# ViT block with experts on one core: second statistics on ScalarE, a new hand-written order of units, products on a constant at two waits

## What is computed

```python
h = tokens(x)                              # 16x16 patches @ W + b, a class token, position codes
h = h + attn(layernorm(h))                 # linear attention with running sums (cumsum) over the tokens
u = layernorm(h)
gates = softmax(u @ w_router + b_router); topv, topi = top_k(gates, 2)
pos = cumsum(one_hot(topi)) - 1; keep = pos < cap          # cap = 185 tokens per expert
buf[e, pos] += u[token]                    # gather the tokens of each expert
out = gelu(buf @ w1[e] + b1[e]) @ w2[e] + b2[e]
h = h + sum(w * out[e, pos]) / sum(w)      # w = the gates of the choices that are kept
```

## Time and profile before

| | us |
|---|---|
| three runs, median (lowest, highest) | 168.11 (167.69, 168.73) |
| profiled execution, its own time | 169.34 |
| profiled execution, span from the first to the last instruction | 167.5 |
| busy: TensorE, VectorE, ScalarE, GpSimd | 157.5, 111.4, 77.4, 51.7 |

### The profile page before, as it was taken

The page is one execution under the profiler, slowest core; times in us unless marked ns, Lnnn a source line. Parts: engine busy times, 40 slices in busy tenths (PEclk is TensorE's granted clock), DMA queues, the critical chain, the costliest instruction groups (busy, mean ns, idle before and its releaser), DMA issues.

```text
span 167.5 us, 3069 instructions
## 1 busy us (share of the span) xinstructions
PE 157.5 (94%) x1041; PEld 148.2 (88%) x1041; DVE 111.4 (67%) x361; ACT 77.4 (46%) x186; POOL 51.7 (31%) x51
## 2 busy tenths in 40 slices
PE   7999999999999789989989999999999999999960
PEld 7679999986886689979989999999999999999950
DVE  0077673688588998396948876948669486694620
ACT  4306543526452309343705737657365583655300
POOL 2006213043021000000721735627266272703351
PEclk9999999999999955899999999999999999999995
DMA  5999930096014410620158789887888868820422
GB/s 164 429 411 420 386 125 0 9 337 206 0 29 134 122 45 4 195 59 4 45 175 308 144 287 268 248 266 137 287 253 255 263 145 276 245 22 6 46 25 22
DMA packets 17264, 28.48 MB, mean 170 GB/s; under 512 B 1289, under 2 KB 13875, under 8 KB 17125
## 3 DMA queue, kind: packets, MB, share of 16 engines
q1 hardware_dynamic: 14789, 25.48, 45.2%
q0 software_dynamic: 2464, 2.86, 10.0%
HBM read 24.20 MB, written 4.14 MB: 169 GB/s over the span
## 4 chain that ended last, share of the span: by engine, by line
PE 77%; DVE 14%; issue 2%; POOL 2%; DMA 1%; POOLq 1%; DVEq 0%
PE ps L1170 21%; PE ps L1193 11%; PE ps L1091 7%; PE ps L1076 6%; PE ps L1030 6%; PE ps L1195 5%; PE ps L1011 4%; DVE prod L777 2%; DVE z_s L775 2%; PE ps L1203 2%; PE ps L1042 2%; DVE onehot L752 2%; PE ps L1180 2%; PE ps L1158 2%; DMA rows_in<-xrows,src_row 1%
## 5 line engine op out<-in xcount | busy, mean ns | idle before, releaser
L475 POOL DMA_INDIRECT out_rows<-out_s,dst_row x16 | 23.7, 1483 | 40.4 <-ACT out_s L620 34.1
L596 ACT ACTIVATE first_t<-ps,b_cur 128x186 f32<-128x186 f32 x64 | 23.1, 412 | 25.5 <-PE ps L1170 25.5
L1193 PE MATMUL ps<-hid_hl,split 128*128 128x372 f32 x96 | 29.0, 369 | 0.0
L460 POOL DMA_INDIRECT rows_in<-xrows,src_row x14 | 15.7, 1124 | 33.2 <-DVE src_row L868 29.2
L1195 PE MATMUL ps<-hid_hl,split 128*128 128x186 f32 x96 | 23.9, 249 | 0.0
L1170 PE MATMUL ps<-first_t,w_even 128*128 128x186 f32 x128 | 21.8, 322 | 0.7 <-DVE first_t L890 0.7
L1170 PE MATMUL ps<-first_t,patch_t 128*128 128x186 f32 x128 | 21.6, 321 | 0.0
L899 DVE CAST hid_hl<-first_t 128x372 fp32r<-128x372 f32 x28 | 10.7, 383 | 16.1 <-ACT first_t L596 16.1
L1170 PEld LDWEIGHTS ps<-first_t,w_even 128*128 128x128 f32 x128 | 20.1, 190 | 1.0 <-issue 1.0
L1170 PEld LDWEIGHTS ps<-first_t,patch_t 128*128 128x128 f32 x128 | 20.1, 190 | 0.0
L1195 PEld LDWEIGHTS ps<-hid_hl,split 128*128 128x128 f32 x96 | 18.3, 191 | 0.0
(11 more groups left out here) (165 smaller groups left out, 272.9 us busy)
## 6 DMA issues: line engine op xcount, KB each, us to landing
w_even<-w SPq DMA_DIRECT2D x8, 1024.0 KB, 5.3
patch_t<-w SPq DMA_DIRECT2D x8, 1024.0 KB, 5.3
patch_t<-patches SPq DMA_DIRECT2D x2, 972.0 KB, 11.2
att<-attn SPq DMA_DIRECT2D x1, 1280.0 KB, 8.4
first_t<-first SPq DMA_DIRECT2D x1, 870.0 KB, 6.0
xrows<-xn SPq DMA_DIRECT2D x3, 288.0 KB, 2.4
out_rows<-h SPq DMA_DIRECT2D x3, 288.0 KB
first_t<-first SPq DMA_DIRECT2D x1, 580.0 KB, 4.2
```

Of the source, the lines that this page charges most:

```text
L460: pool.indirect_dma_start(out=rows_in[q][0:SIZES[s], s, :], out_offset=None, in_=xrows[:, :], in_offset=bass.IndirectOffsetOnAxis(ap=src_r ...
L475: pool.indirect_dma_start(out=out[:, :], out_offset=bass.IndirectOffsetOnAxis(ap=dst_row[0:SIZES[s], c:c + 1], axis=0), in_=out_s[q][0:SIZ ...
L596: ins = act.activation(hid[:, f, :], bank(pair)[:, (f % 2) * SL:(f % 2 + 1) * SL], ACT.Gelu, bias=b1_cur[q][:, f:f + 1])
L1193: pe.matmul(dst[:, 0:2 * SL], w2_h[q][:, f, cols], hid_hl[:, f].rearrange("p a s -> p (a s)"), start=f == 0, stop=False)
```

## The change

- The mean of the second normalisation comes from the router product: `wr_c` has a ninth column of 1/256, set by GpSimd, and `means2` on VectorE copies nine columns per tile to `read_s`. The sum of squares about that mean comes from ScalarE: one ACTIVATE Square per tile with `accum_out` (`squares2`), whose elements go to `xn` and are overwritten by `rows2`. `root2` takes it with a scale of 1/256. `bn_stats` and `bn_aggr` of norm2 are gone.
- `UNITS`, the PSUM slots, `DVE_ORDER`, `ACT_ORDER` and GpSimd's order are new. norm2 E comes before norm2 C, both before slots 0. pick 0 and pick 1 are units in slot 0.
- `rows2` and `keep2` count as two steps; SyncE stores `xn` and `h2` each after its own, in ScalarE's order.
- Four products on the constant stand before slots 0, three before pick 0 (`bridge`).
- pick 1 runs over its five tiles for the first half of the features, then for the second; each half is signalled.
- In expert 0 the look-up of ids comes after pair 2; down half 1 is cut after six of its eight blocks, and the look-up of weights and `turn_in` stand in the cut. The biases of expert 0 are copied at the start.

The diff, cut to its core:

```diff
+BRIDGES = {('slots', 0): 4, ('pick', 0): 3}
...
+READ = NE + 1
...
-        UNITS = [("proj", A, 0), ("mac", 0, 1), ("uw", 0, 2), ("proj", B_, 3), ("norm1", A, 0), ("proj", C, 2),
-                 ("norm1", B_, 3), ("xn_t", A, 0), ("proj", E, 1), ("zc", A, 3), ("norm1", C, 2), ("norm1", E, 0),
-                 ("xn_t", B_, 1), ("a", A, 3), ("zc", B_, 1), ("y", A, 3), ("xn_t", C, 2), ("a", B_, 1),
-                 ("norm2", A, 3), ("xn_t", E, 1), ("y", B_, 2), ("zc", C, 1), ("norm2", B_, 2), ("zc", E, 1),
-                 ("a", C, 0), ("a", E, 1), ("y", C, 3), ("y", E, 1), ("norm2", C, 1), ("slots", 0, 3),
-                 ("norm2", E, 0), ("slots", 1, 2)]
-        PLACE = {(kind, n): u for u, (kind, n, _) in enumerate(UNITS)}
-        PICK_SLOT = 3
-
-
-        DVE_ORDER = [("proj", A), ("uw", 0), ("stats1", A), ("rstd1", A), ("proj", B_), ("stats1", B_), ("rstd1", B_),
-                     ("proj", C), ("xn_low", A), ("proj", E), ("sums", A), ("stats1", C), ("stats1", E), ("rstd1", C),
-                     ("prod", A), ("sums", B_), ("add_up", A), ("rstd1", E), ("prod", B_), ("stats2", A), ("rstd2", A),
-                     ("add_up", B_), ("sums", C), ("stats2", B_), ("sums", E), ("prod", C), ("rstd2", B_), ("prod", E),
-                     ("add_up", C), ("add_up", E), ("choose", 0), ("stats2", C), ("place", 0), ("count", 0),
-                     ("stats2", E), ("rstd2", C), ("rstd2", E), ("choose", 1), ("place", 1), ("count", 1), ("know", 0),
-                     ("know", 1)]
-        ACT_ORDER = [("mac", 0), ("root1", A), ("m_high", 0), ("norm1", A), ("root1", B_), ("xn_high", A), ("norm1", B_),
-                     ("xn_copy", B_), ("root1", C), ("norm1", C), ("root1", E), ("xn_copy", C), ("norm1", E),
-                     ("xn_copy", E), ("root2", A), ("norm2", A), ("root2", B_), ("norm2", B_), ("root2", C), ("root2", E),
-                     ("rows2", C), ("rows2", E), ("keep2", C), ("keep2", E)]
+        UNITS = [("proj", A, 0), ("mac", 0, 1), ("uw", 0, 2), ("proj", B_, 3), ("norm1", A, 0), ("proj", C, 1),
+                 ("norm1", B_, 2), ("proj", E, 3), ("norm1", C, 0), ("xn_t", B_, 1), ("norm1", E, 2), ("xn_t", A, 3),
+                 ("zc", B_, 1), ("zc", A, 3), ("a", A, 0), ("a", B_, 2), ("xn_t", E, 1), ("xn_t", C, 3), ("y", B_, 2),
+                 ("zc", C, 1), ("norm2", B_, 3), ("y", A, 0), ("a", E, 2), ("zc", E, 1), ("norm2", A, 0), ("a", C, 1),
+                 ("y", E, 3), ("y", C, 2), ("norm2", E, 1), ("norm2", C, 3), ("slots", 0, 2), ("pick", 0, 0),
+                 ("slots", 1, 2), ("pick", 1, 0)]
+        PLACE = {(kind, n): u for u, (kind, n) in enumerate(unit[:2] for unit in UNITS if unit[0] != "pick")}
+        PICK_SLOT = 0
+
+
+        DVE_ORDER = [("proj", A), ("uw", 0), ("stats1", A), ("proj", B_), ("rstd1", A), ("proj", C), ("stats1", B_),
+                     ("rstd1", B_), ("proj", E), ("stats1", C), ("stats1", E), ("rstd1", C), ("xn_low", A), ("rstd1", E),
+                     ("sums", B_), ("sums", A), ("prod", B_), ("prod", A), ("add_up", B_), ("sums", C), ("means2", B_),
+                     ("add_up", A), ("rstd2", B_), ("sums", E), ("prod", E), ("means2", A), ("prod", C), ("add_up", E),
+                     ("rstd2", A), ("add_up", C), ("means2", E), ("choose", 0), ("means2", C), ("rstd2", E), ("place", 0),
+                     ("count", 0), ("rstd2", C), ("choose", 1), ("place", 1), ("count", 1), ("know", 0), ("know", 1)]
+        ACT_ORDER = [("mac", 0), ("m_high", 0), ("root1", A), ("norm1", A), ("root1", B_), ("norm1", B_), ("xn_copy", B_),
+                     ("root1", C), ("xn_high", A), ("root1", E), ("norm1", C), ("norm1", E), ("xn_copy", E), ("xn_copy", C),
+                     ("squares2", B_), ("keep2", B_), ("root2", B_), ("rows2", B_), ("squares2", A), ("root2", A),
+                     ("keep2", A), ("rows2", A), ("squares2", E), ("keep2", E), ("root2", E), ("squares2", C), ("root2", C),
+                     ("keep2", C), ("rows2", E), ("rows2", C)]
+        POOL_ORDER = (B_, A, C)
...
-                return ("keep2", n) if n in (C, E) else ("norm2", n)
+                return max(("rows2", n), ("keep2", n), key=ACT_ORDER.index)
             return LAST_READ[kind], n
 
-        READS = [last_read(kind, n) for kind, n, _ in UNITS]
+        READS = [last_read(kind, n) for kind, n, _ in UNITS if kind != "pick"]
+        READS += [step for step in ACT_ORDER if step[0] in ("rows2", "keep2") and step not in READS]
...
-            for g, (t0, n) in enumerate(GROUPS):
-                drained(sp, "norm2", g)
-                store_rows(xrows, xn, t0, n, rows_stored[g])
-                store_rows(out, h2, t0, n, out_stored)
+            for step in ACT_ORDER:
+                if step[0] == "rows2":
+                    done(sp, step)
+                    store_rows(xrows, xn, *GROUPS[step[1]], rows_stored[step[1]])
+                elif step[0] == "keep2":
+                    done(sp, step)
+                    store_rows(out, h2, *GROUPS[step[1]], out_stored)
...
+            pool.memset(wr_c[:, :, NE:], 1.0 / D).then_inc(pool_set, 1)
...
+            pool.wait_ge(m_split, 3)
+            for n in POOL_ORDER:
...
+                pool.wait_ge(scaled, POOL_ORDER.index(n) + 1)
...
+                    act.wait_ge(squared, nth(ACT_ORDER, ("squares2",), ("squares2", g)))
+                    for r, a, b in parts:
+                        ins = act.activation(std[0:r, base + a:base + b], squares[0:r, a:b], ACT.Sqrt,
+                                             bias=eps_col[0:r], scale=1.0 / D)
                 ins.then_inc(std_ready, 1)
+
+            def sum_squares(g):
+
+                act.wait_ge(means_read, nth(DVE_ORDER, ("means2",), ("means2", g)))
+                drained(act, "xn_t", g)
+                p = slot("norm2", g)
+                t0, n = GROUPS[g]
+                for i in range(n):
+                    t = t0 + i
+                    r = rows_of(t)
+                    ins = act.activation(xn[0:r, t], p[0:r, i * D:(i + 1) * D], ACT.Square, bias=read_s[0:r, t, NE:],
+                                         scale=-1.0, accum_out=squares[0:r, t:t + 1])
+                ins.then_inc(squared, 1)
...
-                drained(act, "xn_t", g)
-                normalise(slot("norm2", g), g, NT)
+                normalise(slot("norm2", g), g, NT).then_inc(act_drained, 1)
 
             def keep2(g):
+                act.wait_ge(means_read, nth(DVE_ORDER, ("means2",), ("means2", g)))
...
-            act.wait_ge(picked, 1)
+            act.wait_ge(picked, KD)
...
+            def means2(g):
+
+                t0, n = GROUPS[g]
+                p = filled(dve, "norm2", g)
+                for r, a, b in tile_parts(t0, t0 + n):
+                    raw = p[0:r, 3 * D + (a - t0) * READ:3 * D + (b - t0) * READ]
+                    ins = dve.tensor_copy(read_s[0:r, a:b], raw.rearrange("p (t e) -> p t e", e=READ))
+                ins.then_inc(means_read, 1)
+                dve.wait_ge(means_read, nth(DVE_ORDER, ("means2",), ("means2", g)))
...
+            dve.tensor_copy(b1_cur[0][:, :], b1_t[:, 0:KF])
+            dve.tensor_copy(b2_cur[0][:, :], b2_t[:, 0:KD]).then_inc(biases_ready, 1)
...
+                if not first:
+                    load_biases(e, q)
+
+            def load_biases(e, q):
...
-                if g == 0:
-                    drained(pe, "slots", 0)
                 t0, c = CHOICES[g]
-                for t in range(t0, t0 + c):
-                    for m, (first, _n) in enumerate(GROUPS):
-                        if t == first:
-                            drained(pe, "norm2", m)
-                    pe.wait_ge(onehot_ready, t + 1)
-                    r = rows_of(t)
-                    for k in range(KD):
-                        ins = pe.matmul(pick_slot[:, k, :], xn[0:r, t, k * 128:(k + 1) * 128],
-                                        onehot[0:r, t, :], start=t == 0, stop=t == NT - 1)
-                return ins
+                last = t0 + c == NT
+                for halves in ([[k] for k in range(KD)] if last else [range(KD)]):
+                    for t in range(t0, t0 + c):
+                        for m, (first, _n) in enumerate(GROUPS):
+                            if t == first:
+                                done(pe, ("rows2", m))
+                        pe.wait_ge(onehot_ready, t + 1)
+                        r = rows_of(t)
+                        for k in halves:
+                            ins = pe.matmul(pick_slot[:, k, :], xn[0:r, t, k * 128:(k + 1) * 128],
+                                            onehot[0:r, t, :], start=t == 0, stop=t == NT - 1)
+                    if last:
+                        ins.then_inc(picked, 1)
...
+            def bridge(products):
+
+                drained(pe, *[unit[:2] for unit in UNITS if unit[2] == PICK_SLOT and unit[0] != "pick"][-1])
+                for _ in range(products):
```

(48 more changed lines are left out.)

50 lines of the change are left out of this document (27 added, 23 removed).

## The result

| | before | after |
|---|---|---|
| median (lowest, highest), four runs each | 168.38 (167.69, 168.73) | 163.32 (163.20, 163.92) |
| profiled execution, its own time | 169.34 | 163.92 |
| its span | 167.5 | 162.1 |

The ratio is 0.970, 95% interval 0.966 to 0.974: 5.1 us less. The forecast was 162.3 us for the median and 163.5 for the profiled execution.

A forecast was written before the change was run, and what follows sets the result against it. It took TensorE, busy 94% of the span, as the bound, with a halved clock from 58.0 to about 68.2 us. Terms -1.0 + 0 - 4.5 + 0.5 + 0 - 0.8 = -5.8 gave 163.5 us profiled, 162.3 median; range 161.1 to 166.4.

The forecast's parts named there:

- The front: Attention units up to the last y: the new order covers TensorE's waits for VectorE, -1.0 us.
- a sign of being wrong: VectorE idle before rstd2 C or rstd2 B, waiting for ScalarE's root, would show the forecast wrong; no size given.
- The last y to expert 0: Choice of experts and first pick: -4.5 us, about 2.9 from the clock, the rest a shorter wait and other halved records.
- +0.5 for Square: Second statistics on ScalarE: each Square taken as 0.60 us, low end 0.455, delaying C's root and rstd2 C by 0.5 us.
- Rival 2: ScalarE becomes the bound if a Square takes 0.75 to 1.0 us: 163.4 to 166.1 us, chance 0.07.
- Rival 1: The clock falls again during 3.0 us of transposes and nine-column products, then constant products: 163.7 to 167.1 us, chance 0.22.
- The last pick by halves, 0: Pick 1 by halves gains 0: VectorE copies the first half late, and ScalarE's half waits for the second.
- Expert 0, -0.8: Expert 0 reordered: waits for marks and gathered rows end, 0.93 us, less a new tail; -0.8, between -0.9 and -0.4.
- The tail: End of expert 0: two blocks, 0.65 us, cover VectorE's copy of buffer 1 and its wait; costs 0.15 us.
- The later experts, 0: From 88.4 us on, seven TensorE-bound experts stay fixed; a 1 us delay of expert 2's weights is absorbed.
- Rivals 3 and 4: Third: Square and Sqrt need table loads, 169.0 us, 171.5 with fallen clock, chance 0.05. Fourth: order does nothing, chance 0.08.
- Rival 4: The order does nothing: new waits eat the front, pick gains only the clock; -3.2, 164.9 us, chance 0.08.

The follow-up runs named there:

- e3: Changed kernel with the second normalisation's statistics back on VectorE and no Square on ScalarE; 168.10 us, ratio 0.996 to the kernel before.
- e11: e3 with eight constant products, instead of four and three, at the waits before slots 0 and pick 0; 166.74 us, ratio 0.989 to the kernel before.
- e2: Kernel before with constant products added at its waits alone (five before norm2 C, three before slots 0, five before pick 0); 166.48 us, ratio 0.988 to it.
- e9: Changed kernel with each group's Squares done twice on ScalarE, the first time into spare space; 166.35 us, ratio 0.989 to the kernel before.
- e1: Changed kernel without the constant products before slots 0 and pick 0; 165.87 us, ratio 0.987 to the kernel before.
- e4: Changed kernel with the last pick run tile by tile for both halves and signalled once at its end; 163.87 us, ratio 0.971 to the kernel before.
- e7: Changed kernel with VectorE's buffer copies moved ahead: expert 0's before find_slots(0, 3), expert 1's before reading the coefficients; 163.95 us, ratio 0.971 to the kernel before.
- e12: e7 with ScalarE's Gelu table load moved behind its half of the buffer of expert 0; 163.54 us, ratio 0.971 to the kernel before.
- e10: Kernel before with only expert 0 in the new order; 168.60 us, ratio 0.999 to the kernel before.
- e6: Changed kernel with expert 0 in the order of before; 163.45 us, ratio 0.969 to the kernel before.
- e8: Changed kernel with SyncE not waiting for the gathered rows before sending for the weights of expert 2; 163.96 us, ratio 0.974 to the kernel before.

## Why the prediction was right

**The front, -1.0.** Measured -1.20, in every profile of the new order with the statistics on ScalarE and the Squares done once (27.31 or 27.32). Part of it needs these statistics: with them on VectorE it is 28.07 to 28.09 (e3, e11). The wait of 0.29 us at rstd2 B, named as a sign of being wrong, is there, but the stage is shorter than forecast all the same.

**The last y to expert 0, -4.5 and +0.5 for Square.** Measured -4.11, so the sum of the two was right. That is partly luck, because two misses cancel. The clock's share is 2.5, not 2.9 (e2). Square costs 0.46 us start to start, my low end, not 0.60: the read of the accumulator lies beside the next Square. By the walk that is worth 0, not +0.5; no run prices it alone. Rival 2 has its mechanism confirmed, while its condition did not come true: e9 shows what 0.9 us per tile costs. The walk gave 3.2 us for it, the profile 3.3.

**The clock holds.** The granted clock stayed full, and e1 shows what for: without the products it falls, and the stage grows by 1.7 us. Rival 1 was near. The 3 us of transposes and nine-column products, of which no row of before had an example, went by at the full clock, in e1 too; there the clock fell after that stretch had been followed by waits of 0.97 and 0.70. (My count of three slices with a lower clock in the earlier trace rows left out the span's last one, which lies far behind this stage.)

**The last pick by halves, 0.** Measured 0 (e4). I gave two reasons: VectorE comes late, and ScalarE's half waits for the second half anyway. e7 and e12 took the first away and gained nothing, so the second is enough by itself.

**Expert 0, -0.8.** This step failed. The stage fell by 0.57 in the two profiles of the changed kernel, likewise in e9, e10 and e11, and by nothing in e1, e3 and e4, where VectorE wakes 0.6 us behind the weights look-up. The two waits that the new order ends were worth 0.80, not 0.93: that is the stage of e7 (12.83), which has no tail. The tail, VectorE's copy behind the last two blocks, I had named and priced at 0.15; it takes 0.23, or 0.8 where VectorE wakes late. In the time the new expert 0 is worth nothing: undoing it costs nothing (e6), doing it alone gains nothing (e10).

**The later experts, 0.** "A delay of 1 us is absorbed" was wrong. In the profile before, ScalarE waits for no weights of an expert. In both profiles of the changed kernel it waits twice, 0.58 and 1.02 us, 0.27 and 1.10. Over all profiles a wait of up to 0.72 us left no expert above 10.47, and one of 0.89 or more stood with an expert of 10.59 or more, so what is absorbed is about 0.7. The w2 behind the wait of 1.02 took 7.2 us to land where 5.3 is the median of the earlier trace rows. The stage to the end grew by 0.45 and 0.51. Of that 0.12 to 0.14 lies in expert 1, which takes 10.44 to 10.47 in most profiles with the new expert 0 and 10.32 to 10.35 in those with the old one (before, e2, e6), and the rest in the late expert. That these transfers run late is shown. Why they do is open: a late expert comes with the old expert 0 as well (e6), and with e10 in the old order, so neither the place of turn_in nor the order of units explains it alone. A guess that I didn't test is the time at which the weights, the gathers and the adds of the output meet in the queues. e8 moved one of the meetings and had no late expert, but neither had e1, e3, e4, e9 and e11, so it says little.

**From the profile to the median.** In the profiled executions the span fell by 5.4 for 5.8 (163.92 for 163.5): 0.2 better in the front and 0.1 between the last y and expert 0, then 0.2 worse in expert 0 and 0.45 in the later ones. The median missed by 1.0. Of the other 0.6, 0.27 is the median before, which is 168.38 with a fourth run, not 168.11, and 0.36 is a step of the sum that doesn't hold: I took a gain read in one profiled execution off the median. The one before lay 0.96 us above its median of four, the one after 0.60.

**Rivals 3 and 4.** No table load stands between Square and Sqrt. The Trainium skill's sentence on cheap functions ("ScalarE: Activation LUTs", section on table sets) names relu, copy, identity and abs, and not square, so that Square and Sqrt need no load between them is told by this trace alone. The Trainium skill's rate of one element per cycle and lane whatever the function ("ScalarE: Activation LUTs", section on the pipeline for one element) agrees with Square's price, 0.46 us by the row beside 0.455 for the normalise of the same shape. Rival 4, pick gets the clock and the order nothing, is what e11 and e2 show for the order alone; the order and the statistics together give 2.8 us beyond the clock (42.11 for 44.94).

## What to carry to other kernels

Walk the old and the new order by one rule and compare stages, not absolute times; the differences came out within 0.2 us here for the two stages that gained most. Reordering may pay only together with moving work between engines: here the order alone gave nothing (e11). Where TensorE waits inside a stretch of short products, a few products on a constant can be worth nearly as much as that rearrangement (2.5 us of the stage for 2.8), if they fit in waits that are there anyway. What is won just ahead of a steady loop may be given back by its transfers: look at how near each of them lands to its use before counting the gain. And compare a variant with a run of its own group: 0.6 us of one stage between e4 and the changed kernel did not come from e4's edit.

## What the runs showed that I had not expected

- An ACTIVATE with an accumulator output has a second row, the read of the accumulator, 0.19 to 0.21 us long. To an ACTIVATE that doesn't need the sum it costs no time: the next Square starts 0.09 us behind the read's start (47.08 after 46.99). A root that needs the sum starts 0.59 us behind the last Square instead of 0.45.
- VectorE starts 0.04 us behind the last row of the weights look-up in most profiles of the new expert 0 and 0.6 in those of the first group, while it is never over 0.05 behind the look-up of ids. No row shows by what.
- Transfers of 1 MB of weights landed in 5.2 us and in 8.2 within the same loop (e7).
- The dip of the clock lasted about 10 us before, 3.4 in e1 and 6.8 in e3. It began 4.2 us ahead of the first product of pick 0 before, 2.0 ahead in e3 and 1.3 behind it in e1, and ended in all three while the products of pick 0 ran.
